# One stage of a fused two-layer graph kernel, its side steps placed one unit earlier in the program

## The reference, cut to what matters

```python
def _L0_gnn_ref(z, dist_matrix, W, B):
    msg = z @ W + B
    sens = exp(-(1.0 / r - 1.0 / mu) ** 2 / (2.0 * sigma * sigma))      # mu 1, sigma 0.5
    weights = jnp.where(dist_matrix < CUTOFF, sens, 0.0)                # CUTOFF 1
    return weights @ msg

def _L1_gnn_ref(x, adj, W):
    A_hat = adj + jnp.eye(adj.shape[0], dtype=adj.dtype)
    d_inv_sqrt = jnp.sum(A_hat, axis=1) ** (-0.5)
    A_norm = d_inv_sqrt[:, None] * A_hat * d_inv_sqrt[None, :]
    support = x @ W.T
    out = A_norm @ support
    return jax.nn.relu(out)

h = jnp.maximum(_layernorm(x, axis=-1), 0.0)
x = x + _L0_gnn_ref(h, adj, L0_gnn_W, L0_gnn_B)
h = jnp.maximum(_layernorm(x, axis=-1), 0.0)
x = x + _L1_gnn_ref(h, adj, L1_gnn_W)
```

## Time and profile before

| | |
|---|---|
| median of 3 runs | 589.21 us (588.77 to 590.28) |
| the profiled execution | 589.94 us |
| its span on the core | 588.2 us |
| busy: PE, DVE, ACT, POOL | 529.9, 468.5, 462.3, 58.9 us |
| granted TensorE clock, mean | 0.971 |

### The profile page before, as it was taken

How to read it: one execution, slowest core, us unless ns; L and a number is a source line. 1 busy time by engine, 2 the same in 40 slices (tenths; PEclk the granted TensorE clock), 3 DMA queues, 4 the chain that set the end, 5 groups by cost and what they waited for, 6 DMA issues and landing times.

```text
span 588.2 us, 4967 instructions
## 1 busy us (share of the span) xinstructions
PE 529.9 (90%) x1579; PEld 239.1 (41%) x1579; DVE 468.5 (80%) x532; ACT 462.3 (79%) x305; POOL 58.9 (10%) x100
## 2 busy tenths in 40 slices
PE   1559797989989999999999898999998999999994
PEld 0344333323434444344444344444443444445442
DVE  2899988998999898999999799995999469203155
ACT  1399899999899899998999969999599946910010
POOL 3973300000000000000000000000000001101000
PEclk9859898989989999999999999999999999999999
DMA  9999999999998999779979978998686230948122
GB/s 214 242 325 320 372 351 366 363 306 323 359 340 200 289 320 281 227 240 347 241 195 319 264 213 235 344 254 236 143 214 144 76 138 17 421 145 295 53 71 72
DMA packets 90652, 145.19 MB, mean 247 GB/s; under 512 B 10369, under 2 KB 81282, under 8 KB 81666
## 3 DMA queue, kind: packets, MB, share of 16 engines
q1 hardware_dynamic: 83376, 105.94, 64.7%
q0 software_dynamic: 5808, 38.28, 18.6%
q10 hardware_dynamic: 1442, 0.66, 0.5%
HBM read 106.04 MB, written 38.80 MB: 246 GB/s over the span
## 4 chain that ended last, share of the span: by engine, by line
PE 46%; ACT 24%; DVE 19%; issue 6%; DMA 2%; POOL 1%; ACTq 1%; DVEq 0%
PE acc L411 17%; PE mix L434 13%; PE mix L424 9%; DVE kept L690 7%; ACT wt L565 6%; ACT wt L570 6%; ACT wt L575 6%; ACT wt L584 5%; DVE wt L705 4%; DVE rowpart L698 3%; DMA x<-in_x_dram 2%; PE acc L434 2%; PE mix L442 2%; PE side L434 1%; DVE wt L711 1%
## 5 line engine op out<-in xcount | busy, mean ns | idle before, releaser
L411 PE MATMUL acc<-wt,msg 128*128 128x512 f32 x512 | 238.2, 609 | 12.3 <-ACT wt L584 7.1
L411 PEld LDWEIGHTS acc<-wt,msg 128*128 128x128 f32 x512 | 96.1, 194 | 145.6 <-issue 124.9
L690 DVE STREAM_TRANSPOSE kept<-raw 128x2048 f32<-128x2048 f32 x64 | 147.5, 2304 | 0.6 <-DMA raw<-in_adj_dram 0.4
L705 DVE SCALAR_TENSOR_TENSOR wt<-kept 128x2048 f32<-128x2048 f32 x64 | 146.5, 2290 | 1.7
L565 ACT ACTIVATE wt<-wt 128x2048 f32<-128x2048 f32 x64 | 121.7, 1902 | 15.4 <-DVE wt L705 15.2
L570 ACT ACTIVATE wt<-wt 128x2048 f32<-128x2048 f32 x64 | 121.6, 1899 | 0.5
L424 PE MATMUL mix<-kept,support 128*128 128x512 f32 x224 | 101.3, 595 | 3.5 <-ACT mixed L626 1.8
L584 ACT ACTIVATE wt<-wt 128x2048 f32<-128x2048 f32 x50 | 94.9, 1899 | 0.0
L575 ACT ACTIVATE wt<-wt 128x2048 f32<-128x2048 f32 x50 | 94.8, 1897 | 0.0
L434 PE MATMUL mix<-late,support 128*128 128x512 f32 x208 | 93.4, 593 | 1.3 <-DVE support L806 1.3
L698 DVE TENSOR_REDUCE rowpart<-raw 128x16 f32<-128x4096 f32 x16 | 70.1, 4380 | 0.0
(11 more groups left out here) (91 smaller groups left out, 266.8 us busy)
## 6 DMA issues: line engine op xcount, KB each, us to landing
raw<-in_adj_dram SPq DMA_DIRECT2D x512, 128.0 KB, 6.4
adj_t_spill<-kept SPq DMA_DIRECT2D x35, 1024.0 KB, 9.1
late<-adj_t_spill POOLq DMA_DIRECT2D x26, 1024.0 KB, 8.3
raw<-adj_t_spill POOLq DMA_DIRECT2D x9, 1024.0 KB, 9.8
out_dram<-kept SPq DMA_DIRECT2D x32, 64.0 KB, 1.8
x<-in_x_dram POOLq DMA_DIRECT2D x24, 64.0 KB, 7.1
x<-in_x_dram ACTq DMA_DIRECT2D x8, 64.0 KB, 4.5
w_sb<-in_L_gnn_W_dram ACTq DMA_DIRECT2D x1, 64.0 KB
```

Of the source, the lines that this page charges most:

```text
L411: mm = nc.tensor.matmul(acc0[:], msg[:, col(u) * T + k, :], wt[:, u % WTS, k, :], start=(first and k == 0), stop=(last and k == T - 1))
L690: nc.vector.transpose(dst, src).then_inc(turned, 1)
L705: nc.vector.scalar_tensor_tensor(out=wt[:, u % WTS], in0=v, scalar=CUTOFF, in1=v, op0=ALU.is_lt, op1=ALU.mult).then_inc(cut_done, 1)
```

## The change

Three tables or conditions move; nothing is computed that was not before.

- `STEPS` now has three columns: turns 1 to 3, turn 4, turns 5 to 7. The last two are the numbers of before. In turns 1 to 3 `turn_hid` goes from index 4 to 3, `multiply_support` from 5 to 4, `make_support` from 5 to 4. `copy_hid` keeps index 3, but in these turns the group stands behind `log` and ahead of `square`, `invert` and `weigh` instead of behind them. `turn_hid` stands ahead of the unit's `multiply_weights`.
- The `mix_once` of a turn's last unit (15, 23, 31, 39, 47) stood at the end of that unit. It now stands in the next turn at index 1, behind `multiply_weights` and `turn_sums`.
- The jobs (0,0), (0,1), (1,1), (0,2), (1,2), (2,2) go from units 15, 24, 26, 32, 33, 34 to 13, 21, 22, 30, 31, 33.

```diff
-JOBS = {15: [(0, 0)], 24: [(0, 1)], 26: [(1, 1)],
-        32: [(0, 2)], 33: [(1, 2)], 34: [(2, 2)],
+JOBS = {13: [(0, 0)], 21: [(0, 1)], 22: [(1, 1)],
+        30: [(0, 2)], 31: [(1, 2)], 33: [(2, 2)],
...
+LAST_MIX_TURNS = 5
...
+FIRST_TURNS = 3
 EARLY_TURNS = 5
-STEPS = {"own_rows": (2, 3), "copy_x1t": (1, 2), "turn_x1": (2, 3), "make_x1": (3, 4), "copy_hid": (3, 4),
-         "turn_hid": (4, 5), "multiply_support": (5, 6), "make_support": (5, 7), "sum_quads": (1, 1)}
+STEPS = {"own_rows": (2, 2, 3), "copy_x1t": (1, 1, 2), "turn_x1": (2, 2, 3), "make_x1": (3, 3, 4),
+         "copy_hid": (3, 3, 4), "turn_hid": (3, 4, 5), "multiply_support": (4, 5, 6), "make_support": (4, 5, 7),
+         "sum_quads": (1, 1, 1)}
 
 def step_at(g, idx, name):
-    return g >= 1 and idx == STEPS[name][g >= EARLY_TURNS]
+    return g >= 1 and idx == STEPS[name][0 if g <= FIRST_TURNS else 1 if g < EARLY_TURNS else 2]
...
@@ PE
-                if step_at(g, idx, "turn_hid"):
+                if step_at(g, idx, "turn_hid") and g > FIRST_TURNS:
                     turn_hid(g - 1)
...
+                if 2 <= g <= LAST_MIX_TURNS + 1 and idx == LAG - 1:
+                    mix_once(g * G - 1)
+                if step_at(g, idx, "turn_hid") and g <= FIRST_TURNS:
+                    turn_hid(g - 1)
...
-                if g >= 1 and idx == G - 1:
+                if g > LAST_MIX_TURNS and idx == G - 1:
                     mix_once(u)
...
@@ ACT
                 log(u)
+                if step_at(g, idx, "copy_hid") and g <= FIRST_TURNS:
+                    log_pows(g - 1)
+                    copy_hid(g - 1)
+                    exp_pows(g - 1)
...
-                if step_at(g, idx, "copy_hid"):
+                if step_at(g, idx, "copy_hid") and g > FIRST_TURNS:
                     log_pows(g - 1)
                     copy_hid(g - 1)
                     exp_pows(g - 1)
```

## The result

The kernel after takes 600.08 us (median of 3 runs, 599.28 to 600.89), the kernel before 589.21; the ratio is 1.0174 [1.0154, 1.0195]. The profiled execution is the one of 600.08, its span 598.3 us, its mean granted clock 0.967. I had forecast slower, at 592.6, with a range up to 595.3. The direction is right, the size is not: 10.9 us instead of 3.4.

The account below looks back on a forecast made before the run. No engine alone bounds it: ACT and DVE, then PE, then DVE, then ACT. Delays of turns 1 to 3 reach 3.4 us at turn(35), everything later 0: 593.3 profiled, 592.6 median, own range 590.7 to 594.3, wider 587.0 to 595.3.

Parts of the forecast that it names:

- What bounds the kernel: Whole kernel: ACT and DVE to about 165 us, PE to 228, DVE to 302, then ACT; PE waits 2.59 at 330.19.
- Step 1: Turns 1 and 2, support and copies one unit up: log(13) 2.5 us late, quad(17) about 2.1, quad(19) 2.4.
- Step 2: Turn 3, last mix and jobs: mix_once(23) holds turn(27), 4.0 us late; quad(31) 3.0 late, turn(35) 3.4 late.
- What costs nothing: Earlier jobs (0,2), (1,2), (2,2), mixes 39 and 47 in PE's 2.59 us wait: 0; POOL's loads at worst 1 us.
- The low clock: Turn 2: PE's product of unit 19 behind a wait might run slow, adding 1.7 us, 5.1 in all; 3.4 taken.
- faster: Turn 3: turn(27) not held, loop steps hide, DVE starts turn(30) 2.7 us earlier; 586.5 us, chance 0.17.
- No change: PE bounds 165 to 228 us, holds on DVE cost only its 2.75 us wait; 589.2 to 590.6 us, chance 0.20.

Follow-up runs that it names:

- mixes 39 and 47 back: The kernel after with mixes 39 and 47 returned to the end of their own unit; 594.61 us, ratio 1.0087.
- jobs only: The kernel before with only the six jobs moved one to three units up; 592.05 us, ratio 1.0029.
- 39 moved, product put in: The kernel before with mix 39 moved behind the next turn's sums and job (1,3) one unit earlier; 594.03 us, ratio 1.0065.
- turn 5 filled: The kernel before with job (3,3) and turn_x1(4) put ahead of the weight product of unit 40; 586.12 us, ratio 0.9924.
- only 15, 23, 31 moved: The kernel before with only mixes 15, 23 and 31 moved behind the sums of the next turn; 594.63 us, ratio 1.0082.
- support at 5: The kernel after with mixes 39 and 47 in their old place and make_support at index 5 in turns 1 to 3; 593.41 us, ratio 1.0060.
- steps only: The kernel after with all jobs and mixes put back, only support chain and copies one unit up in turns 1 to 3; 596.84 us, ratio 1.0120.
- support product up: The kernel before with multiply_support(2) put ahead of the weight product of unit 26 in turn 3; 589.58 us, ratio 0.9989.
- before again: The kernel before run again with nothing changed; 593.45 us, one run.
- 39 and 47 behind the first product: The kernel before with mixes 39 and 47 moved behind the first weight product of the next unit; 593.39 us, ratio 1.0056.

## Why the prediction was wrong

- *What bounds the kernel*: right up to turn 4. The chain on ACT and DVE, then PE, then DVE is what the steps show. Wrong was what I took from the wait at 330.19: that PE has 2.59 us to give in turn 5.
- *Step 1*: right. turn(13) 2.4 late net of the start (forecast 2.6), turn(21) 4.2 (4.3), log(21) at 174.73 (174.2), with the wait of 1.46 us for cut.
- *Step 2*: right. turn_sums(2) 205.77 (205.3), turn(27) held 1.75 us to 210.37 (209.7), turn(29) 227.02 (226.4), turn(30) 231.57 (230.95), quad(31) 249.97 (249.4), turn(35) 266.42 (265.6). Each is 0.5 to 0.8 late, most of it the start, which I had left out of the sum. That the total came so near has luck in it: the profile that I started from carried two low-clock products that the kernels after need not have. Against the three kernels without them (turn(35) at -1.7) the change with mixes 39 and 47 back costs 5.0 us by turn(35), not 3.4. The wait of 2.50 us at the end of turn 1 was not in the sum either.
- *What costs nothing*: this step failed, in the sentence "The mixes 39 and 47 one unit later are covered by the 2.59 us that PE waits anyway". I had looked at where the product goes to and not at what it leaves. It leaves PE's place ahead of the weights of unit 38, where ACT sets the time; there the wait grows from 0.83 to 4.26 us. A product of 3.43 us doesn't fit into 2.76 either. That is 0.7 us in turn 5 with the clock up. In turn 6 PE had no wait to give at all. The step that I had called covered measures 6.0 us: 3.3 and 2.7.
- *The low clock*: I had priced it at 1.7 us for turns 1 and 2 and at nothing for turn 5, since there was no new wait in my picture of it. Of the 3.3 us of turn 5 it is 2.75. The Trainium skill (TensorE: Matmul & The Clock Gate, HAM oscillation — how this bites in real kernels) says that waits between bursts of products bring PE back to the low clock. The product behind 4.26 us agrees, in the three profiles that have such a wait (6.46, 6.53, 6.53). For the waits of 2.1 to 2.7 us the runs show both levels, the wait of 2.6 us for one and the same program too. There the sentence of the page settles nothing, and the measured products are what can be said.
- *The rivals*: "faster" fell where I had put its test, turn(27) started at 210.37 and not by 206. "No change" fell with quad(29) waiting 1.03 us for ACT.
- *Also missed*: DVE held at turn(43) and turn(51), the longest new waits of the profile. They turned out to cost nothing: with the first taken away the loss of turn 5 stayed, and at the second PE had lost all of its time before DVE was released.

Open: what the jobs alone cost (592.05, expected 587.8 or 591.0). By turn(35) their profile is 0.2 ahead of the profile of before, but 1.5 behind the three kernels that had the early products at full clock too; the 1.6 us after that are the product of unit 40 at the low clock, which the kernel before has at times as well. Open too is whether the three slower runs of "39 moved, product put in" were slow by the clock alone.

## What to carry to other kernels

A product that is moved leaves a hole: look first at what its engine will wait for where it stood, and only then at the wait that it is to fill. An engine's wait for another engine's result is not stock to be spent elsewhere, since filler ahead of a later wait can't come from a place ahead of an earlier one without opening that. Work taken from behind the wait can fill it, as turn 5 filled showed. A long wait that the page shows on an engine (here 6.6 us of DVE) is no cost until a kernel without it is faster, or until what follows is seen to be late by it.

## What the runs showed of the hardware

Whether a product behind a wait of 2.1 to 2.7 us runs at 1.2 or 2.4 GHz is not fixed by the program. The product of unit 40, behind a wait of 2.59 or 2.60 us, took 3.67 us in four profiles (before, 39 and 47 back, only 15, 23, 31 moved, support at 5) and 5.12 to 5.37 in four others (steps only, jobs only, support product up, before again). That of unit 12, behind 2.15 us, took 5.40 and 6.70 in the two profiles of the kernel before, 5.28 to 5.40 in four kernels that are the same up to there, and 3.70 in three more (39 and 47 behind the first product, support product up, turn 5 filled); with that of unit 18 this makes the 1.6 us by which the turn(27) of these three is early in the table. That of unit 14, behind 2.50 us, took 5.11 in the kernel after and 3.70 in the one with mixes 39 and 47 back. The kernel before shows it in its times: its runs on the same chip as the last experiments group by mean granted clock, 588.6 to 589.1 us at 0.974 to 0.980, 589.4 to 591.3 at 0.971 or 0.972, 592.6 to 593.1 at 0.968. (On another chip one run at 0.968 took 589.54, so the mean clock does not fix the time.) So this kernel has a spread of 4.5 us with nothing changed, and a sum made against one profile carries that profile's share of it. One wait of 3.33 us was followed by a product of 3.70 us, one of 3.98 by 5.40 (steps only), those of 4.26 by 6.46 and 6.53: longer waits cost more often and more, but these are five products in all, and the runs settle no more than that.
